# Window attention: one matmul per head and sub-block, for the head's own ten scores and all values

## What is computed

```
x = concat(center, neigh - center)          # per point and neighbour, 4 orderings: 256 values
x16 = float16(x); qh = x16.reshape(B*N, 10, 8 heads, 32)
scores = einsum('bihd,bjhd->bhij', qh, qh) / sqrt(32)
out = einsum('bhij,bjhd->bihd', softmax(scores), qh)     # then out @ W_lin.T + b_lin, a second linear map,
                                                          # instance norm, leaky ReLU, maximum over neighbours
```

## Time and profile before

| | us |
|---|---|
| median of 3 runs | 2311.37 |
| the three runs | 2306.75, 2311.55, 2311.37 |
| span of the profiled execution (the page gives no other time for it) | 2306.2 |
| busy in that span: PE, DVE, ACT, POOL | 1865.0, 1904.0, 1616.7, 1007.8 |

### The profile page before, as it was taken

How to read it: one execution, slowest core, us unless ns; L and a number is a source line. 1 busy time by engine, 2 the same in 40 slices (tenths; PEclk the granted TensorE clock), 3 DMA queues, 4 the chain that set the end, 5 groups by cost and what they waited for, 6 DMA issues and landing times. The chain is left out here.

```text
span 2306.2 us, 99850 instructions
## 1 busy us (share of the span) xinstructions
PE 1865.0 (81%) x37528; PEld 1286.8 (56%) x37528; DVE 1904.0 (83%) x3658; ACT 1616.7 (70%) x3249; POOL 1007.8 (44%) x995
## 2 busy tenths in 40 slices
PE   0296665888888566499999998677999999999967
PEld 0023335777777344389999997343554544454432
DVE  6798986999999599689989987783888888888865
ACT  0299985888888699689999998456555555555532
POOL 0000006999999200178888886001434444444311
PEclk9997668999999666699999999799999999999979
DMA  2103766666565167655555552212322322222210
GB/s 59 14 1 89 165 163 141 123 122 123 122 123 121 32 157 166 157 110 109 107 105 110 108 105 53 93 28 67 92 83 73 91 74 81 79 85 82 61 56 19
DMA packets 435513, 216.09 MB, mean 94 GB/s; under 512 B 301259, under 2 KB 404843, under 8 KB 435304
## 3 DMA queue, kind: packets, MB, share of 16 engines
q1 hardware_dynamic: 430120, 210.73, 39.2%
q10 hardware_dynamic: 5312, 4.31, 0.8%
HBM read 161.97 MB, written 52.96 MB: 93 GB/s over the span
## 5 line engine op out<-in xcount | busy, mean ns | idle before, releaser
L865 PE MATMUL pQ<-QM,QX 128*128 128x64 f16 (+1 forms) x5760 | 531.5, 216 | 2.1 <-issue 2.1
L863 PE MATMUL pQ<-neigh_lo,QX 128*128 128x32 f16 (+1 forms) x5760 | 519.8, 188 | 2.1 <-issue 2.1
L863 PEld LDWEIGHTS pQ<-neigh_lo,QX 128*128 128x128 f16 x5760 | 494.9, 103 | 5.4 <-issue 2.8
L865 PEld LDWEIGHTS pQ<-QM,QX 128*128 128x128 f16 x5760 | 486.9, 104 | 1.8 <-issue 1.7
L961 POOL TENSOR_TENSOR Dm<-Sc,mx 128x450 f32<-128x450 f32 x384 | 365.8, 953 | 77.8 <-DVE mx L921 77.8
L968 POOL TENSOR_TENSOR Ap<-E,R 128x450 f32<-128x450 f32 x384 | 366.0, 953 | 67.9 <-DVE R L934 57.5
L998 ACT ACTIVATE Vs<-pQ 128x480 f32<-128x480 f32 (+1 forms) x384 | 295.6, 770 | 4.7 <-PE pH L891 3.0
L930 DVE STREAM_TRANSPOSE AT<-Ap 128x480 f32<-128x480 f32 x384 | 259.3, 675 | 33.4 <-PE pH L891 10.9
L1963 POOL TENSOR_TENSOR MT<-cb,decay 128x512 f32 (+1 forms) x128 | 164.0, 1302 | 247.4 <-PEq L1731 150.6
L1011 ACT ACTIVATE E<-Dm 128x450 f32<-128x450 f32 x384 | 224.1, 584 | 60.1 <-POOL Dm L961 60.0
L921 DVE TENSOR_REDUCE mx<-Sc 128x15 f32<-128x450 f32 x384 | 224.0, 583 | 15.2 <-ACT Sc L992 15.1
(11 more groups left out here) (362 smaller groups left out, 3584.5 us busy)
## 6 DMA issues: line engine op xcount, KB each, us to landing
QM<-scratch_q SPq DMA_DIRECT2D x192, 240.0 KB, 2.7
QX<-scratch_q SPq DMA_DIRECT2D x768, 60.0 KB, 2.5
scratch_q<-QT SPq DMA_DIRECT2D x120, 360.0 KB, 4.8
Wg<-in_in_proj SPq DMA_DIRECT2D x64, 256.0 KB, 2.7
Wh<-in_in_proj SPq DMA_DIRECT2D x64, 256.0 KB, 2.8
Wo<-in_out_proj SPq DMA_DIRECT2D x64, 256.0 KB, 2.6
W_s<-in_in_proj SPq DMA_DIRECT2D x16, 256.0 KB, 2.7
CT<-scratch_c SPq DMA_DIRECT2D x192, 11.2 KB, 2.2
```

The source lines that it names most:

```text
L863: nc.tensor.matmul(pQ[:, p, u // PB, o + 32:o + BW], qx[u], W["neigh_lo"][:, 0:O], start=False, stop=True, skip_group_check=True)
L865: last = nc.tensor.matmul(pQ[:, p, u // PB, o:o + BW], qx[u], qm[u], start=False, stop=True, skip_group_check=True)
```

## The change

- The score matmuls. Each sub-block takes four matmuls, one per head, with a 30-column query (rows: 32 dimensions x 3 points on 96 partitions, zero except for the own point; all 32 dimensions once more on the last 32) as weights, and 10 + O columns as the other operand: the head's keys of the own point and, beside them in the same tile QW, the value weights (coarse part on the first 96 rows, remainder on the last 32). That makes 60 matmuls per item in place of 30 and the masks; the masks and `neigh_lo` are gone. The outputs are 32-partition strips. The ten columns of a score row are all there is, so Dm and E are 150 columns wide.
- In each run of SW = 16 elements the 15 sub-blocks lie side by side (one is padding), so the operands of one sub-block are read with a step of 16 f16 elements, 32 bytes. Before it was 3 elements.
- The difference Dm moves from POOL to DVE and reads PSUM. DVE's maximum reads PSUM too. ACT's copy Sc is gone. E is taken at lag 1, Z, R and A at lag 2, the transpose at 3, the mix at 4, Hs, square and hmax at 5. POOL spreads R over the three points (RM) before it multiplies.
- SP loads two items with five DMAs: QW (96 partitions, 240 KB in runs of 320 B), three of QX (80 KB each in runs of 320 B), one of QX (240 KB in runs of 960 B). The load of CT follows at lag 0 behind its wait on `mixed`.
- Layer 1 loops over 8 steps, layer 2 over 6, with that many items in QW, QX, CT, AT and Vs; pH has 2 buffers in layer 1 and 1 in layer 2.
- At the start of a layer the value weights are copied into all buffers of QW by DVE, POOL and ACT, more is set to zero, and six matmuls of zeros clear pQ. In `gather_windows` QT's layout follows, with five subtractions per batch for four, and each centre store writes runs of 90 B, 384 per DMA.

The diff, cut to its core; of the lines that are taken away most are left out, since they stand in the functions printed above.

```diff
+SW = 16
+GQ = SUBS * K
+GW = SW * K
+UT = 2
 NSUB = (N - LEAD) // PTS + 2
 GC = 32 * SUBS
-RES = 3
...
+            c16 = scratch["c16"].rearrange("(m c) (a g s x) -> m s c a g x", m=2, s=SL, g=GROUPS, x=GP)
             a = bass.ds(r * (4 // SL) + k // SL, 1)
+            eng.dma_start(c16[m, k % SL][:, a, :, :].rearrange("c a g x -> c (a g) x"),
+                          cen16[m * C:(m + 1) * C, k, :].rearrange("c (g x) -> c g x", x=GP)).then_inc(q_out[k], 16)
...
+            q16 = scratch["q16"].rearrange("(a g s) (c m) x -> m s c a g x", m=M, g=GROUPS, s=SL)
             a = bass.ds(r * (4 // SL) + k // SL, 1)
+            eng.dma_start(q16[m, k % SL][:, a, :, :].rearrange("c a g x -> c (a g) x"),
+                          QT[m * C:(m + 1) * C, k, :, :, :, :].rearrange("c g n j u -> c g (n j u)"))\
+                .then_inc(q_out[k], 16)
...
+                    ahead = LEAD * K + HALF - 1
                     for n in range(PTS):
+                        v.tensor_tensor(QT[:, k, 0:LAST, n, :, 0:SUBS],
+                                        rows(ext, k, ahead + n, (GP, LAST), (1, K), (PTS, SUBS)),
+                                        rows(cen, k, n, (GP, LAST), (0, K), (PTS, SUBS)),
                                         ALU.subtract).then_inc(q_v, 1)
+                    v.tensor_tensor(QT[:, k, LAST, :, :, 0:REST],
+                                    rows(ext, k, ahead + GP * LAST, (1, PTS), (1, K), (PTS, REST)),
+                                    rows(cen, k, GP * LAST, (1, PTS), (0, K), (PTS, REST)),
+                                    ALU.subtract).then_inc(q_v, 1)
                     dve.wait_ge(q_v, b * QV + 5 * QV - 1)
+                    v.tensor_tensor(QT[:, k, 0, :, :, 0:2], rows(ext, k, 0, (K, PTS), (1, K), (PTS * K, 2)),
...
-    U = RV = 8
-    NQ = 8
+    U = (8, 6)[O // C - 1]
+    NP = (2, 1)[O // C - 1]
+    ND = (4, 3)[O // C - 1]
+    NU = U // UT
+    NH = U // SL
+    RV = NA = U
+    NB = 3
+    PB = SUBS // NB
+    ON = K + O
+    LOADS = 16 * 5
...
+        QX = sb("QX", [128, NU, UT * 4, PTS, GW], F16)
+        QW = sb("QW", [128, NU, UT * 4, ON * SW], F16)
+        CT = sb("CT", [128, NU, UT * GP], F16)
...
+        def weights_of(k):
+
+            y = k % UT * 4
+            to = QW[:, k // UT, y:y + 4, K * SW:].rearrange("p h (o u) -> p h o u", u=SW)
+            return to, W["stack"][:, :, :].unsqueeze(3).to_broadcast([128, 4, O, SW])
...
-                if at(4) and k % 2 == 0:
-                    (t, r), k = at(4), (k - 4) % U
+                if at(0) and k % UT == 0:
+                    (t, r), w = at(0), k // UT
+                    first = isinstance(t, int) and t < U
+                    span = bass.ds(t * 4, UT * 4)
+                    sp.wait_ge(projected, t + UT)
+                    sp.dma_start(QW[0:96, w, :, 0:GW], rows[:, span, :]).then_inc(q_in[w], 16)
+                    if first:
+                        sp.wait_ge(zeroed[w], 1)
+                    for n in range(PTS):
+                        sp.dma_start(QX[n:96:PTS, w, :, n, :], q16[:, span, n, :]).then_inc(q_in[w], 16)
+                    sp.dma_start(QX[96:128, w, :, :, :].rearrange("p y n x -> p y (n x)"),
+                                 q16[:, span, :, :].rearrange("d y n x -> d y (n x)")).then_inc(q_in[w], 16)
+                    if first:
                         sp.wait_ge(ct_zeroed, 1)
+                    sp.wait_ge(mixed, pack(r, k + UT - 1) + 1)
+                    sp.dma_start(CT[0:2 * C, w, :], c16[:, bass.ds(r * NU + w, 1), :].rearrange("p v x -> p (v x)"))\
+                        .then_inc(c_in[w], 16)
 
...
+            none = A[:, 0:2, :].rearrange("p k x -> p (k x)").bitcast(F16)
+            for p in range(2):
+                for b in range(NB):
+                    nc.tensor.matmul(pQ[:, p, b, :], none[:, 0:128], none[:, 0:512], start=True, stop=True)
+            pe.wait_ge(rows_zeroed, 1)
 
             def scores(k, at):
                 if at(0):
+                    (t, r), p, w = at(0), k % 2, k // UT
+                    if isinstance(t, int) and t < U and k % UT == 0:
+                        pe.wait_ge(placed[w], UT)
+                    pe.wait_ge(q_in[w], r * LOADS + LOADS)
+                    pe.wait_ge(shifted, t + 1)
                     pe.wait_ge(vs_ready, t + 1)
                     for u in range(SUBS):
+                        for h in range(4):
+                            y = k % UT * 4 + h
+                            query = QX[:, w, y, :, :].rearrange("p n (j u) -> p u (n j)", u=SW)[:, u]
+                            both = QW[:, w, y, :].rearrange("p (x u) -> p u x", u=SW)[:, u]
+                            at0 = u % PB * ON
+                            last = nc.tensor.matmul(pQ[32 * h:32 * h + PTS * K, p, u // PB, at0:at0 + ON], query, both,
+                                                    start=True, stop=True)
                     last.then_inc(projected, 1)
...
-                if at(5) and (k - 5) % SL == SL - 1:
-                    t, r = at(5)
+                if at(4) and (k - 4) % SL == SL - 1:
+                    t, r = at(4)
+                    k3 = (k - 4) % U
...
+            for w in range(0, NU, 2):
+                v.memset(blank(w), 0.0).then_inc(zeroed[w], 1)
+                if w == 0:
+                    v.memset(QW[96:128, :, :, 0:GW].rearrange("p w y x -> p (w y) x"), 0.0).then_inc(rows_zeroed, 1)
+            for k in range(1, U, 3):
+                v.tensor_copy(*weights_of(k)).then_inc(placed[k // UT], 1)
...
             def step(k, at):
                 if at(1):
+                    (t, _), p = at(1), (k - 1) % U % ND
+                    dve.wait_ge(projected, t + 1 + U)
+                    v.tensor_reduce(banks(mx[:, p, :], 1)[:, :, :, 0], results((k - 1) % 2)[:, :, :, 0:K], X, ALU.max)\
+                        .then_inc(max_ready, 1)
+                if at(2):
+                    (t, _), p = at(2), (k - 2) % U % ND
                     dve.wait_ge(exped, t + 1 + ND)
-                if at(4):
-                    (t, r), k5 = at(4), (k - 4) % U
+                    v.tensor_reduce(Z[:, p, :], subs(E[:, p, :], K), X, ALU.add).then_inc(summed, 1)
+                if at(1):
+                    (t, _), p = at(1), (k - 1) % U % ND
+                    dve.wait_ge(max_ready, t + 1)
+                    dve.wait_ge(exped, t + 1)
+                    v.tensor_tensor(banks(Dm[:, p, :], K), results((k - 1) % 2)[:, :, :, 0:K],
+                                    banks(mx[:, p, :], 1).to_broadcast([128, NB, PB, K]),
+                                    ALU.subtract).then_inc(shifted, 1)
...
+                if at(5) and (k - 5) % SL == SL - 1:
+                    (_, r), k5 = at(5), (k - 5) % U
+                    q, p = pack(r, k5), k5 // SL % NH
+                    dve.wait_ge(copied, q + 1 + NP)
+                    dve.wait_ge(squared, q + 1 + NH)
...
                     pool.wait_ge(r_ready, t + 1)
+                    nc.gpsimd.tensor_tensor(RM[:, p, :, :], R[:, p, :].unsqueeze(2).to_broadcast([128, SUBS, PTS]),
+                                            own[:, :].unsqueeze(1).to_broadcast([128, SUBS, PTS]),
+                                            ALU.mult).then_inc(rm_ready, 1)
+                    pool.wait_ge(rm_ready, t + 1)
                     pool.wait_ge(turned, t + 1 + NA - ND)
+                    nc.gpsimd.tensor_tensor(subs(A[:, p, :], 32)[:, :, 0:PTS * K].rearrange("p s (n j) -> p s n j", n=PTS),
+                                            subs(E[:, p, :], K).unsqueeze(2).to_broadcast([128, SUBS, PTS, K]),
+                                            RM[:, p, :, :].unsqueeze(3).to_broadcast([128, SUBS, PTS, K]),
                                             ALU.mult).then_inc(probs, 1)
...
+                if at(5) and (k - 5) % SL == SL - 1:
+                    (t, r), k5 = at(5), (k - 5) % U
+                    q = pack(r, k5)
+                    rows = pH[:, k5 // SL % NP, 0:GC].rearrange("p (s x) -> p s x", x=32)[:, :, 0:PTS * K]
+                    act.wait_ge(mixed, q + 1 + U // SL)
+                    act.wait_ge(hmax_done, q + 1)
+                    nc.scalar.activation(Hs[:, k5 // SL % NH, :].rearrange("p (s x) -> p s x", x=PTS * K), rows, ACT.Copy,
+                                         accum_out=stat[:, 0, bass.ds(q, 1)]).then_inc(copied, 1)
                 if at(1):
+                    (t, _), p = at(1), (k - 1) % U % ND
+                    act.wait_ge(shifted, t + 3)
+                    act.wait_ge(probs, t + 1)
+                    nc.scalar.activation(E[:, p, :], Dm[:, p, :], ACT.Exp, scale=32.0 ** -0.5).then_inc(exped, 1)
                 if at(1):
                     (t, r), p, kv = at(1), (k - 1) % 2, (k - 1) % U
```

292 lines of the change are left out of this document (97 added, 195 removed).

## The result

| | us |
|---|---|
| before, median of 4 runs | 2309.72 |
| after, median of 4 runs (2689.74 to 2705.69) | 2696.87 |
| ratio after to before | 1.168, 95% interval 1.165 to 1.171 |
| span of the profiled execution after | 2691.5 |

The kernel is slower, as forecast, but by 387 us where I had put 39; the time lies outside the range. The windows of the changed kernel answer to the earlier trace rows: layer 1, layer 2, gathering (busy us and instructions of PE, PEld, DVE, ACT, POOL; granted clock, DMA share, GB/s).

The account below looks back on a forecast made before the run. Waits in in-order queues were taken to bound it: SP's loop in layer 1, ACT and DVE's in layer 2. 13 + 17 + 7 (ends) + 2 (gathering) = 39 us on the 2311.37 median gave 2350 us; range 2280 to 2435.

Parts of the forecast that it names:

- the loop through SP's queue: Layer 1: CT's wait for the mix holds back later loads; 8.5 us per four items, 2.12 against 2.05 each, 13 us.
- Layer 2's loop of ACT and DVE: Layer 2: exponential, values, square, hmax, maximum and difference in a ring; 2.43 us per item against 2.34, 17 us slower.
- The rival in which the sums decide: Both layers: buffers cover the waits, the busiest queue sets 1.66 us per item; 2114 us, chance 0.12.
- the price of the score matmuls: PE, both layers: 60 score matmuls of one item take 0.65 us, from 10 ns each in the mix's f32 rows.
- the rival's sign: 60 score matmuls taking 0.9 us and more in the profile after would show PE slower than forecast.
- The rival: PE slower through operands read at 32-byte steps: scores doubled to about 0.93 and 1.3 us; 2383 us, chance 0.22.
- the rival's sum: Slower PE: SP loop 9.1 us in layer 1 and 9.8 in layer 2; 2311 + 42 + 21 + 9 = 2383 us.
- the landing path: SP's loads, from a mix's end through CT, five DMA starts and landing to PE: 5.8 us.
- The upper bound that I gave for the landing: Landing of a 240 KB DMA, taken as 2.7 us, could be 3.7, adding 0.25 us per item.
- beside ACT's 50 of 50: Gathering: the fifth subtraction and the 90 B stores are covered by busy ACT; 2 us, between 0 and 10.
- The clock's fall, priced in a rival: Within the slower-PE rival (0.22): at 1.2 GHz the mix costs up to double, layer 1 2.6 us per item, 2445 us.
- the layers' ends: Starts and ends of both layers: zeroing and copies on DVE against shorter lags; 7 us, between 0 and 14.

Follow-up runs that it names:

- ct_late: Changed kernel with the centres' load (CT) issued four items later in SP's queue; 2522.47 us, ratio 1.090 to before.
- before_ct_early: Kernel before with its centres' load issued with the pair's QM and QX instead of four items later; 2506.42 us, ratio 1.084.
- all_three: Changed kernel with CT's load four items later, score-and-value operands at unit step, and gathering subtractions in the earlier order, written without gaps; 2364.85 us, ratio 1.025.
- three_loads: Changed kernel with the three QX loads to every third partition made one load to 96 neighbouring partitions; 2663.50 us, ratio 1.155.
- both edits: Changed kernel with CT's load four items later and both score-and-value operands read at unit step; 2410.74 us, ratio 1.045.
- gather_packed: Changed kernel with the gathering's QT subtractions reading in the order of the kernel before and writing without gaps; 2665.06 us, ratio 1.153.
- the unit step: Changed kernel with both operands of each score-and-value matmul read at neighbouring elements instead of a step of 16; alone 2557.69 us, ratio 1.107.

## Why the prediction was wrong

**Direction and mechanisms: right.** The change ties queues that were loose, and the loop through SP's queue holds as it was put: CT 0.18 us after a mix, QX releasing PE after some 4 us once per four items in layer 1 (at the pair between it waits under 1 us), POOL and DVE far from full. ct_late and before_ct_early show that the wait alone makes it, in either kernel. Layer 2's loop of ACT and DVE, 2.43 us, was measured at 2.42 as soon as nothing slower hid it, link by link. The rival in which the sums decide is out: even all_three stays at 2.17 and 2.45 us.

**The step that failed first: the price of the score matmuls**, "I take 0.65 in both layers". They cost 1.3 to 1.4 us in layer 1 and 2.15 in layer 2, above the 0.9 that I had named as the rival's sign. I carried 10 ns over from the earlier trace rows, which has the strips and the count but reads adjacent elements. The rival had the right cause and took twice the base, 0.93 and 1.3 us, from f32 matmuls of the weights' folding, where 140 of 216 ns don't depend on the columns. What such a row couldn't show is what four strips in turn pay for each column read at this step: 0.45 ns per matmul. The measured loop in the rival's sum would have said so: with 2.8 and 4.3 us for two items the same four-item loop is 5.8 + 2.8 + 1.35 = 9.95 us in layer 1 and 11.45 in layer 2, 2.49 and 2.86 us per item, 2311 + 84 + 100 + 9 = 2504 us. With it I would have been short by 193 us and not by 347. (The rival's own sum for layer 1 is 5.8 + 1.86 + 1.35 = 9.0 us, not 9.1.)

**The second: the landing path**, taken as 5.8 us. It is 7.1 in the turn shown and 7.3 on average: five DMAs' starts take 2.72 us in place of 1.94 (each of the three to every third partition is 0.72 us behind the last, where the earlier trace rows has 0.48), and 3.46 in place of 2.8 from the last start to PE. The trace of before had 5.8 for its own 480 KB, and before_ct_early confirms that at 5.76. For 720 KB I had let the shorter time per byte of longer runs stand against the larger count, and they don't cancel. three_loads shows that fewer issues alone don't shorten it; whether the bytes or the shape of the loads set it stays open. The upper bound that I gave for the landing, 3.7, held.

**The third: in layer 2 I named the wrong loop.** With both sizes put right, SP's loop gives 7.1 + 4.3 + 1.45 = 12.9 us for four items, 3.2, above ACT's and DVE's 2.43. That is what the trace shows. ct_late takes it to PE's own 2.94, and only both edits to 2.42.

**The fourth: "beside ACT's 50 of 50"** for the gathering, 2 us. DVE had been busy 46 of 50 us already, and I counted the added subtraction but not that 1650 columns in the new order take 2488 ns where 1710 took 1936. DVE became the bound. gather_packed gives back 32 us, some 5 of them by POOL's zeroing of QT, to which I had given no term.

The clock's fall, priced in a rival, is there: 0.78 in layer 1, and 0.62 with cheaper matmuls in the same loop. It costs through the mix, 1.8 us on average in layer 1 where I had 1.35: 0.45 us in four items, 22 us of the time. The matmuls at a step don't follow it. It is not what makes the kernel slow, since layer 2 has 0.98 and lost more.

**The account.** By the measured paces layer 1 lies 192 x (2.91 - 2.12) = 152 us above the forecast and layer 2 192 x (3.25 - 2.43) = 157. In layer 1 these are, per four items, 1.3 us of scores, 1.5 of the path and 0.45 of the mix: about 60, 70 and 22 us. The 38 us that are left of the 347 lie in the gathering and at the layers' ends; gather_packed gives back 32 of them. The edits say nearly the same: alone they give 139, 174 and 32, all three together 2696.87 - 2364.85 = 332 us. But all_three is not the kernel that I forecast, for ct_late takes away a loop that the forecast had kept, and the unit step makes other values. That it ends 15 us from 2350 proves no more than that nothing large is missing.

No version here beats the kernel before. A layout with neighbouring elements in both operands that still loads in few DMAs wasn't tried; my estimate, from all_three, is some 2365 us, 2.5% behind, as long as ACT and DVE keep their loop.

## What to carry to other kernels

Price a matmul by the bytes between its neighbouring elements as well as by its columns and strips: if no row reads at that step, measure it alone before fusing operands into one tile for it. In a queue that runs in order, ask of every wait what stands behind it that doesn't need it: here the place of one DMA of 11 KB, four items earlier or later, was worth 174 us in one kernel and 196 in the other. And when two loops are close in price, carry both with their bounds to the end, since the second one decides as soon as one term grows.
